# Layers: the first unit's output projection of a group moved from behind the scores of rounds 8 and 9 to behind those of rounds 10 and 11

## The reference

```python
for l in range(DEPTH):                       # DEPTH = 2
    h = shift_token(x)                       # second half of the features taken from the token before
    q, k, v = split(h @ wqkv)                # 8 heads of 64
    q, k = rotary_xpos(l2norm(q) * qs, l2norm(k) * ksc)
    o = local_attention(q, k, v)             # windows of 128 tokens: own window and the one before
    x = x + o @ wo                           # the projection and the residual
    h = shift_token(x)
    h = (h - mean(h)) / sqrt(var(h) + 1e-05) * lg + lb
    a, g = split(h @ w1 + b1)
    x = x + (a * gelu(g)) @ w2 + b2
```

## Time and profile before

| what | value |
|---|---|
| runs | 2183.95, 2188.03, 2192.35 us; median 2188.03 us |
| the profiled execution | 2188.08 us, of which 2186.3 us are the span from the first to the last instruction |
| PE busy | 1866.0 us, 85% of the span |
| DVE, ACT, POOL busy | 1522.5, 1185.1, 985.3 us |
| mean granted TensorE clock | 0.949 of full speed |
| one group, in the first layer | 91.3 us (even number) or 89.2 us (odd) |

### The profile page before, as it was taken

How to read it: one execution, slowest core, us unless ns; L and a number is a source line. 1 busy time by engine, 2 the same in 40 slices (tenths; PEclk the granted TensorE clock), 3 DMA queues, 4 the chain that set the end, 5 groups by cost and what they waited for, 6 DMA issues and landing times.

```text
span 2186.3 us, 36482 instructions
## 1 busy us (share of the span) xinstructions
PE 1866.0 (85%) x12941; PEld 1402.0 (64%) x12941; DVE 1522.5 (70%) x3736; ACT 1185.1 (54%) x2717; POOL 985.3 (45%) x781
## 2 busy tenths in 40 slices
PE   5568999999975899898899988887898998988986
PEld 3444444444433677787777867676786777877776
DVE  2668888777756586775867758585675867758673
ACT  0545555544344655656556566564656556565562
POOL 0325454647464544444434444443544535444451
PEclk7669999999987899999999999999999999999998
DMA  4000000101222000000000001010101000010000
GB/s 143 25 27 27 1 25 10 51 16 51 78 63 78 12 22 17 20 15 21 19 17 21 19 21 52 28 54 24 33 18 31 28 22 25 18 30 28 24 18 22
DMA packets 83406, 68.58 MB, mean 31 GB/s; under 512 B 10852, under 2 KB 79508, under 8 KB 83224
## 3 DMA queue, kind: packets, MB, share of 16 engines
q1 hardware_dynamic: 83224, 66.25, 9.8%
HBM read 45.22 MB, written 16.81 MB: 28 GB/s over the span
## 4 chain that ended last, share of the span: by engine, by line
PE 36%; DVE 19%; issue 7%; ACT 6%; DMA 2%; POOL 1%; SPq 0%; DVEq 0%; ACTq 0%; POOLq 0%
PE bank_O L1243 4%; PE bank_T L1231 3%; PE bank_P L260 3%; PE bank_A L260 3%; ACT share_x L1381 3%; PE bank_A L262 3%; PE bank_A L261 3%; PE bank_P L261 3%; PE bank_A L1220 3%; PE bank_P L262 3%; DVE l_t L1561 3%; DVE share_x L1577 2%; DVE l_u_lo L1642 2%; PE bank_T L1210 2%; PE bank_T L260 2%
## 5 line engine op out<-in xcount | busy, mean ns | idle before, releaser
L1812 POOL TENSOR_TENSOR share_x<-share_x,l_rinv 128x512 f32<-128x512 f32 (+1 forms) x256 | 251.0, 1002 | 374.8 <-DVE l_rinv L1585 374.6
L1800 POOL TENSOR_TENSOR l_t<-share_qk,l_tab 128x512 f32<-128x512 f32 x128 | 175.8, 1397 | 315.5 <-DVE l_ss L1543 310.1
L1381 ACT ACTIVATE share_x<-share_x,l_nb 128x256 f32<-128x256 f32 (+1 forms) x512 | 248.0, 486 | 81.7 <-DVE l_nb L1577 81.5
L260 PE MATMUL bank_A<-l_f_hi,l_w_hi 128*114 128x256 f32 (+1 forms) x768 | 220.4, 287 | 5.9 <-DVE l_f_lo L1622 3.7
L1577 DVE CUSTOM_DVE_ANT_0 share_x<-bank_A,share_scr 128x256 f32<-128x256 f32 (+1 forms) x512 | 177.3, 401 | 57.3 <-PE bank_A L1220 57.1
L262 PE MATMUL bank_A<-l_f_hi,l_w_lo 128*114 128x256 f32 (+1 forms) x768 | 216.3, 282 | 0.0
L261 PE MATMUL bank_A<-l_f_lo,l_w_hi 128*114 128x256 f32 (+1 forms) x768 | 216.2, 282 | 0.0
L1231 PE MATMUL bank_T<-ident,share_x 128*128 128x128 f32 x960 | 147.8, 288 | 66.9 <-POOL share_x L1812 34.4
L645 ACT ACTIVATE pr<-ps_S 128x1024 f32<-128x1024 f32 x128 | 130.7, 1023 | 124.7 <-PE ps_S L539 124.0
L1642 DVE TENSOR_TENSOR l_u_lo<-l_up,l_u_hi 114x256 fp32r<-114x256 f32 (+1 forms) x192 | 196.1, 1028 | 0.1
L895 POOL TENSOR_TENSOR acc<-acc,pr 128x1024 f32<-128x1024 f32 x64 | 155.6, 2432 | 53.0 <-ACT pr L645 48.7
(11 more groups left out here) (269 smaller groups left out, 5132.6 us busy)
## 6 DMA issues: line engine op xcount, KB each, us to landing
l_xs<-x_layers SPq DMA_DIRECT2D x64, 128.0 KB, 2.5
share_x<-in_x SPq DMA_DIRECT2D x8, 512.0 KB, 3.8
base_rows<-share_x SPq DMA_DIRECT2D x16, 256.0 KB, 2.1
x_layers<-share_x SPq DMA_DIRECT2D x16, 256.0 KB, 2.1
l_xs<-x_layers SPq DMA_DIRECT2D x64, 64.0 KB, 2.2
x_layers<-l_yb SPq DMA_DIRECT2D x32, 128.0 KB, 1.8
share_m<-base_rows SPq DMA_DIRECT2D x32, 128.0 KB, 2.9
out<-l_yb SPq DMA_DIRECT2D x32, 128.0 KB, 1.7
```

The lines of the kernel that those rows point to most:

```text
L260: pe.matmul(out, a_hi, b_hi, start=(start and k == 0), stop=False)
L1381: eng.activation(row, row, ACT.Exp, bias=nb[:, R % SS, e:e + 1], scale=-1.0, accum_out=rsum[:, R % SS, e:e + 1]).then_inc(ex_ready, 1)
L1800: eng.tensor_tensor(dst[:, :, :, lo:lo + H2], src[:, :, :, hi:hi + H2], table[:, :, 1, lo:lo + H2].unsqueeze(2).to_broadcast([P, 2, LH, H2 ...
L1812: eng.tensor_tensor(row, row, rinv[:, R % SS, :].unsqueeze(2).to_broadcast([P, 2, P * windows(n)]), ALU.mult).then_inc(pn_ready, 1)
```

## The change

In the queue of PE, `project(first)` moves from the step of rounds 8 and 9 to that of rounds 10 and 11, in front of `h_transpose(following)`. On DVE `residual(first)` moves from behind the minima of round 9 to behind those of round 11, in front of `h_split(following)`, and `moments(first)` moves from slot 0 to slot 1, in front of `moments(first + 1)`. On POOL `x_bias(first)` moves from behind the probabilities of rounds 8 and 9 to slot 0, behind those of rounds 10 and 11. SP's code is unchanged; its `shift(first)` waits for the residual. ACT's is unchanged.

```diff
@@ tensor, loop over r
-                        if r == 8:
+                        if r == 10:
                             project(first)
                         if r == 10 and following < UNITS:
                             h_transpose(following)
@@ vector, loop over r
-                        if r == 9:
+                        if r == 11:
                             residual(first)
-                        if r == 11 and ahead:
-                            h_split(following)
+                            if ahead:
+                                h_split(following)
@@ vector, loop over k
                         if k == 0:
                             residual(first + 1)
-                            moments(first)
                         if k == 1:
                             if ahead:
                                 h_split(following + 1)
-                            moments(first + 1)
+                            moments(first), moments(first + 1)
                             deviation(first // 2)
@@ gpsimd, loop over r
-                        if r == 10:
-                            x_bias(first)
@@ gpsimd, loop over k
-                    if k in (1, 5, 7) and g >= 0:
-                        x_bias(first + 1 + (k - 1) // 3)
+                    if k in (0, 1, 5, 7) and g >= 0:
+                        x_bias(first + (k + 2) // 3)
```

## The result

The changed kernel takes 2213.07 us in the median of four runs (2211.81 to 2216.40), the kernel before 2188.74 in the same comparison; the ratio is 1.012 with a 95% interval of 1.0099 to 1.0140. It is 24 us slower, inside the range of the prediction (2198 to 2232) and 9 us under its value (2222). The profiled execution, the slowest of the four, took 2216.4 us, a span of 2214.6.

The account below looks back on a forecast made before the run. PE was taken to bound the kernel, a group's time being its work plus its waits. 2188.1 us + 15.5 (projection and moments waits) + 18.8 (clock falls) = 2222 us, range 2198 to 2232.

Parts of the forecast that it names:

- First term: Rounds 8 to 12: PE newly waits 0.61 us for POOL in round 7; scores of round 12 start 0.42 us later.
- Scores of rounds 10 and 11 earlier: These scores come at 1092.75 for 1093.73, worth nothing; rival: 0.32 us gained in each of 15 groups, 2183, chance 0.05.
- Second term: Slot 1 on DVE: the second moments push o_split by 0.66 us; PE's slot 2 wait grows from 1.72 to 2.38.
- What costs nothing: x_bias(first), 0.72 us, moves between POOL's idle stretches; SP's later shift and load still land some 3 us before the transposes.
- Third term: Behind PE's lengthened slot 2 wait: half clock in 11 of 15 groups, 1.71 us lost each, 18.8 us.
- 6 of 8 waits elsewhere: From group 7 on, six of eight PE waits of 2.01 to 2.15 us had half clock behind them; basis for 11 of 15.
- The Trainium skill's rule: Only gaps longer than 2.38 us cost the clock; rival: both waits but the clock holds, 2204, up to 2209, chance 0.28.
- Sum: Whole kernel: 2188.1 + 15.5 for both waits + 18.8 for the clock = 2222 us, 1.6% slower.

Follow-up runs that it names:

- e1: Changed kernel with moments(first) put back into slot 0, the rest of the change kept: 2191.10 us, ratio 1.0021 to the kernel before.
- e7: Changed kernel with the next group's input transposes in front of the projection and h_split in front of the residual: 2218.81 us, ratio 1.0140 to the kernel before.
- e2: Kernel before with only moments(first) moved to slot 1: 2213.39 us, ratio 1.0126.
- e9: Changed kernel with moments(first) computed twice in slot 1 and 16 unused transposes ahead of the values of slot 2: 2212.59 us, ratio 1.0122 to the kernel before.
- e3: Changed kernel with 16 unused identity transposes on PE ahead of the values of slot 2: 2202.78 us, ratio 1.0076 to the kernel before.
- e10: Kernel before with 12 unused identity transposes on PE ahead of the values of slot 2: 2188.36 us, ratio 1.0003.
- e4: Kernel before with deviation moved from slot 1 to behind o_split in slot 2: 2160.55 us, ratio 0.9876.

## Why the prediction was right

- **First term, the projection (0.42 us a group, "1092.09 plus the 0.15 us that PE takes after such a release").** Right in its place, too large in size. The transposes of round 7 start 0.49 us later than they could behind those of round 6 (1100.19 against 1099.19 + 0.51, from start to start as in the prediction; the profile's 0.34 counts from the modelled end of the one before), not 0.61. They started 0.07 us after POOL's second multiplication ended (1100.12, half of the four from 1098.10 on), where I had put 0.15. From the end of `o_split` to the scores of round 12 it is 7.83 us in the changed kernel and was 7.56, so 0.27. e1 gives the whole term: ratio 1.0021, with groups 0.25 to 0.3 us longer.
- **Scores of rounds 10 and 11 earlier, worth nothing.** Right. e7 lets the exps of round 11 go 0.75 us earlier, and its groups without a fall are less than 0.1 us shorter.
- **Second term, the moments (0.66 us a group).** Right: 0.69 in the timeline, and e2 shows that the moments alone make nearly the whole loss. e9 over e3 gives 9.8 us for 15 times one more set.
- **What costs nothing.** Right: no wait of PE for a DMA appears, `x_bias` is nowhere waited for, and the load of the next unit was issued at 1109.03, which is 1101.1 in the times of before (group 4 lies 7.96 us later here), in time for its transposes.
- **Third term, the clock (11 falls at 1.71 us).** Right in kind, and shown by e3 with e10 as its control: the fall follows from PE's idling and not from anything else in that slot. The size was 18.8 us in the prediction, too large. Measured are nine falls in the profiled execution at 1.5 us each and not 1.71, 13.5 us, and 10 us in the medians of the change and of e3, some seven falls. The granted clocks of all executions fit this: the clock that PE was not granted, (1 - mean clock) x span, is 121 us in the mean of the change's four executions and 111 to 112 us in those of the kernel before. That 6 of 8 waits elsewhere would carry over to these 15 was a guess, and that it came this near (nine here, eleven in e2) is in part luck. The Trainium skill's rule that only longer gaps would cost the clock (TensorE: Matmul & The Clock Gate, section "HAM oscillation — how this bites in real kernels") would have given 2204; it does not hold here, where the clock fell behind 2.41 us. Whether that wait does it alone is not shown: the 1.48 us wait stands close ahead of it in every group, and no run takes the one away and leaves the other.
- **Sum.** In the profile 13 groups with 0.27 + 0.69 are 12.5 us, groups 7 and 8 add 1.4, the falls 13.5, together 27.4; the span grew by 28.3. The first and third terms were both too large, which is why the value, 2222, lies 9 us over the median, 2213; neither made good the other.

## What to carry to other kernels

An operation is as cheap as the wait that it stands in: two BN operations of 0.6 us were free in one slot, where their engine waited for TensorE, and cost 10 us of waits and 10 to 15 us of clock one slot later, where TensorE waited for their engine. So before moving work of a helper engine, follow the chain from TensorE's longest waits back to their root, and put nothing between the two ends; what already stands there and isn't needed at once (here `deviation`) is the first thing to move, and it gave 27 us. Where a wait of TensorE grows until half clock follows it, the clock can cost more than the added wait (here 1.5 us a fall for 0.69 us of wait), and matmuls without use in that gap can pay.

## What the runs showed of the hardware

That a wait of 2.41 us can cost another 1.5 us through the clock was forecast. By the profiles here, waits of 1.72 us in this place were followed by half clock in none of 15 groups, waits of 2.41 us in nine (eleven in e2), waits of 3.08 us in eleven. How much clock a program loses also changes from one execution to the next, the kernel before included: its mean granted clock was between 0.944 and 0.953, and its time between 2183 and 2193 us. So one profile is a sample.

I had not expected what POOL does to small operations of DVE. Timeline of DVE in e4, the first operations of `deviation` behind `o_split`, and of POOL beside it:

```profile
1105.22 0.56 DVE L1605 TENSOR_SCALAR l_var<-l_mv 128x2 f32<-128x2 f32 x1
1105.82 0.96 DVE L89 TENSOR_SCALAR l_tmp<-l_var 128x2 uint32<-128x2 uint32 x1
1106.82 0.17 DVE L90 TENSOR_SCALAR l_rs<-l_tmp 128x2 int32<-128x2 int32 x1
```

```profile
1104.72 2.04 POOL L1812 TENSOR_TENSOR share_x<-share_x,l_rinv 128x512 f32<-128x512 f32 x2 [4.87 <-DVE l_rinv L1585]
```

Two TENSOR_SCALARs on two elements a partition take 0.56 and 0.96 us while POOL multiplies, and 0.17 once it is done at 1106.76. The first ends with POOL's first multiplication (1105.76), the second with its second. It is so in every group: in e4 the operation of L1605 starts beside POOL 16 times and takes 0.56 us each time, and once without POOL, 0.17. This fits what the Trainium skill (SBUF — State Buffer, section "Who interferes with whom") says of the port pair that the two engines share, held for a whole instruction. It cost `deviation` 1.2 us in e4, which still stayed in front of PE.
